# An adaLN block on eight cores: the first K tile summed chunk by chunk, the modulation rows sent through memory, and the opening loads in another order

## The chip, the cores and the metric

The kernel runs on the 8 cores of one Trainium2 chip. Each core computes one element of the batch with the same program, and nothing passes between cores. The metric is the device time of the slowest core in microseconds (us). Engines are TensorE (PE), VectorE (DVE), ScalarE (ACT), GpSimd (POOL) and SyncE (SP, which only starts transfers here). An MiB below is 1.049 MB.

## The reference, cut to what matters

```python
mod = (silu(c) @ wmod).reshape(8, 6, 1, 1024)
sa, ca, ga, sb, cb, gb = mod[:, 0], ..., mod[:, 5]
ga = sign(ga) * maximum(abs(ga), 0.25)          # gb likewise, sign(0) = 1
h = layernorm(x) * (1 + ca) + sa                # x: 2048 tokens of 1024 per core
q = relu(h @ Wq.T) / 8; k = relu(h @ Wk.T) / 8; v = h @ Wv.T; u = silu(h @ Wu.T)
kv = k.T @ v                                    # per head, 16 heads of 64, over all tokens
x = x + ga * ((rms(q @ kv) * u) @ Wo.T)
h = layernorm(x) * (1 + cb) + sb
x = x + gb * (quantised(h) @ quantised(weight).T * scales + bias)
```

## The kernel before, in words

The 2048 tokens are 16 groups `g` of 128 and four tiles `i` of 512. Work goes in this order: an opening (modulation vectors `sa`, `ca`, and the first tile), then K and V for tiles 0 to 3 with the product `kv` (the first phase), then Q, U, the head outputs and the quantising of the FFN weight for tile 0 (`xunit(0, n)`), and then a loop over the 16 groups with Wo, the second norm and the FFN, in which the next tile's Q and U are mixed in.

No scheduler is at work: each engine has a list (`Queue`) that is filled in program order, and each instruction waits on the semaphores in its `after` arguments. So an instruction that waits holds back all that stands behind it on its engine, and a transfer that waits holds back the later ones of SP or POOL. SP's transfers share one queue, POOL's another. The weights are f32 in memory and are cast to bf16 on the way by POOL's transfers.

The parts that the change touches:

- **Opening.** SP loads eight pieces `wa` of 1 MiB (the `sa` and `ca` columns of wmod for one chunk `dc` of 128 features). `wa_sum(dc)` takes two products with accumulation on DVE. POOL loads x. `xhat(g)` normalises a group: statistics, variance plus epsilon and reciprocal on DVE, square root on ACT, minus mean times 1/std on DVE, then `xh` on ACT. `transp(i, c)` turns it on PE into banks 2 and 3, and an eviction applies `ca`, `sa` into `h1`. For tile 0 the eviction only copies, and `scale(dc)` on DVE applies them when the sums are there.
- **K and V.** `kproj(i, hf, j)` is one unit: 8 matmuls 128x512 over the chunks into one of three banks 4, 5, 6, and an eviction on ACT. Tile 0 takes eight such units, then `transp(1, c)`, then tile 1. `vproj` is the same for V, `kvprod` multiplies into banks 0 and 1.
- **Modulation rows.** `ga`, `sb`, `cb`, `gb` come from 16 pieces of wmod of 1 MiB (`mod_piece`, four for each row), through three stage buffers. DVE sums each piece into `accb`, scaled by a column `silc`. `mod_row` then adds over the partitions with an f32 matmul with ones into bank 7, which also spreads the row over all partitions. The same stage buffers carry Wo (`wo_piece`, which folds `ga` in) and the FFN weight (`ffn_quant`). The list `mods` holds these pieces, and one is taken after every second unit of the first phase and one after every unit in its last eight.
- **Late rows.** `last_rows` and `last_row` make gb times bias, and gb times the weight's scales, the latter with f32 matmuls in the group loop after group 0.

## Time and profile before

| what | value |
|---|---|
| median of three runs | 508.58 us (508.37 to 510.7) |
| profiled execution, device time | 510.15 us |
| its span on the slowest core (core 0) | 508.1 us |
| spans of the other seven cores | 499.9 to 504.5 us |
| granted TensorE clock, core 0 | 0.966 of full speed |
| busy: PE, DVE, ACT, POOL | 405.4, 299.4, 237.8, 57.7 us |
| read from and written to memory | 68.26 MB, 24.64 MB |

A core's span runs from its first to its last instruction. The profiled execution's own time is 2.05 us above the span. Busy is not the same as bounding: what matters is which wait ends last in a stretch, and it changes from stretch to stretch.

### The profile page before, as it was taken

The page shows a single profiled execution, that of the slowest core. Times are in us where ns is not written, and L with a number is a line of the kernel's source. Part 1 is how long each engine was busy: PE and PEld are TensorE (multiplying, and loading weights), DVE is VectorE, ACT ScalarE, POOL GpSimd, SP SyncE. Part 2 cuts the span into 40 slices and gives each one's busy share as a digit, 9 for nine tenths or more (in the row PEclk, how much of TensorE's full clock was granted, in tenths as well). Part 3 has the DMA queues.
Part 4 walks back from the last instruction along what each step waited for, and adds up shares of the span by engine and source line. Part 5 has one row for each costly group of instructions (what it writes and reads, how often), then busy time and mean ns, then how long its engine had stood idle before and what let it go on. Part 6 is the DMA issues. An engine that isn't in the chain of part 4 may idle for free.

```text
span 508.1 us, 6419 instructions; the slowest of 8 cores (499.9 to 508.1 us)
## 1 busy us (share of the span) xinstructions
PE 405.4 (80%) x2028; PEld 189.4 (37%) x2068; DVE 299.4 (59%) x524; ACT 237.8 (47%) x348; POOL 57.7 (11%) x90
## 2 busy tenths in 40 slices
PE   0004568968989999787796989998999989998984
PEld 0002234424544444433442434443444434444441
DVE  0388550184867627446886456663666637665884
ACT  1134165454457323156756385445764367643431
POOL 1021011020000000000002111111201212011321
PEclk9999996999999999999898899998999989999998
DMA  7999969999956665920229950656335752455686
GB/s 189 336 335 192 268 189 234 215 195 265 304 221 195 248 221 183 306 92 1 83 70 301 318 140 10 124 118 119 54 77 90 159 85 55 111 84 124 88 142 143
DMA packets 17984, 84.92 MB, mean 167 GB/s; under 512 B 2336, under 2 KB 2336, under 8 KB 12832
## 3 DMA queue, kind: packets, MB, share of 16 engines
q0 software_dynamic: 7776, 32.51, 33.8%
q1 hardware_dynamic: 10176, 52.01, 31.4%
q8 instruction: 17, 0.28, 0.2%
q14 instruction: 15, 0.12, 0.1%
HBM read 68.26 MB, written 24.64 MB: 183 GB/s over the span
## 4 chain that ended last, share of the span: by engine, by line
PE 51%; DVE 19%; ACT 12%; issue 11%; DMA 4%; POOL 1%; DVEq 1%; SPq 1%; ACTq 0%; POOLq 0%
PE pb L315 43%; DVE junk L454 4%; DVE bn L266 3%; DMA wa<-wmod_a 3%; ACT rn L619 2%; PE pb L380 2%; ACT osq L609 2%; DVE h L705 2%; DMA stage<-wmod_b 1%; DVE am L708 1%; PE pb L617 1%; PE pb L343 1%; ACT xq L719 1%; DVE wm_c L424 1%; ACT rn L622 1%
## 5 line engine op out<-in xcount | busy, mean ns | idle before, releaser
L315 PE MATMUL pb<-wk_s,h 128*128 128x512 bf16 x249 | 62.0, 405 | 9.1 <-DVE h L463 5.8
L315 PE MATMUL pb<-fq,xqT 128*128 128x512 bf16 x247 | 60.5, 385 | 3.4 <-ACT xqT L731 2.2
L315 PE MATMUL pb<-wo_s,u_s 128*128 128x512 bf16 x254 | 61.2, 394 | 1.5 <-DVE u_s L599 1.4
L315 PE MATMUL pb<-h,wu_s 128*128 128x512 bf16 x248 | 60.5, 385 | 0.3
L315 PE MATMUL pb<-h,wq_s 128*128 128x512 bf16 x250 | 60.2, 384 | 0.2
L315 PE MATMUL pb<-wv_s,h 128*128 128x512 bf16 x249 | 59.3, 386 | 0.4
L285 PE MATMUL pb<-id_b,xh 128*128 128x128 bf16 x128 | 13.3, 260 | 49.5 <-ACT xh L275 47.9
L624 DVE SCALAR_TENSOR_TENSOR q_s<-rn,pb 128x512 bf16<-128x512 f32 x32 | 22.0, 687 | 44.6 <-ACT rn L622 42.1
L315 PEld LDWEIGHTS pb<-wk_s,h 128*128 128x128 bf16 x256 | 25.9, 103 | 43.2 <-issue 18.4
L371 DVE SCALAR_TENSOR_TENSOR accb<-stage,silc,accb 128x1024 f32<-128x1024 f32 x28 | 36.0, 1285 | 8.9 <-DMA stage<-wmod_b 6.5
L315 PEld LDWEIGHTS pb<-wo_s,u_s 128*128 128x128 bf16 x256 | 25.7, 101 | 33.4 <-issue 6.4
L338 ACT CAST vT<-pb 128x512 bf16<-128x512 f32 x32 | 18.6, 583 | 41.8 <-PE pb L315 41.8
L330 ACT ACTIVATE kT<-pb 128x512 bf16<-128x512 f32 x32 | 18.7, 592 | 41.1 <-PE pb L315 41.1
L315 PEld LDWEIGHTS pb<-h,wq_s 128*128 128x128 bf16 x256 | 25.2, 99 | 30.4 <-issue 2.5
L315 PEld LDWEIGHTS pb<-fq,xqT 128*128 128x128 bf16 x256 | 24.4, 99 | 31.6 <-issue 6.7
L315 PEld LDWEIGHTS pb<-h,wu_s 128*128 128x128 bf16 x256 | 25.1, 99 | 28.9 <-issue 1.1
L584 ACT ACTIVATE q_s<-pb 128x512 bf16<-128x512 f32 x24 | 14.2, 593 | 45.3 <-PE pb L315 43.8
L315 PEld LDWEIGHTS pb<-wv_s,h 128*128 128x128 bf16 x256 | 24.7, 99 | 28.4 <-issue 3.1
L719 ACT ACTIVATE xq<-h,cst,rs 128x1024 f16<-128x1024 f32 x16 | 19.8, 1239 | 22.4 <-DVE rs L713 22.4
L285 PEld LDWEIGHTS pb<-id_b,xh 128*128 128x128 bf16 x128 | 10.5, 117 | 53.0 <-issue 51.1
L454 DVE SCALAR_TENSOR_TENSOR junk<-wa,silr 128x1024 f32<-128x1024 f32 x16 | 19.6, 1224 | 17.4 <-DMA wa<-wmod_a 16.6
L693 POOL TENSOR_SCALAR ve<-m 128x1 f32<-128x1 f32 x6 | 3.3, 550 | 208.5 <-DVE m L690 208.5
(92 smaller groups left out, 561.1 us busy)
## 6 DMA issues: line engine op xcount, KB each, us to landing
stage<-wmod_b SPq DMA_DIRECT2D x16, 1024.0 KB, 7.0
xr<-x_tm POOLq DMA_DIRECT2D x16, 512.0 KB, 16.6
wa<-wmod_a SPq DMA_DIRECT2D x8, 1024.0 KB, 22.2
xr<-x_tm SPq DMA_DIRECT2D x16, 512.0 KB, 3.6
out_tm<-row_gbb SPq DMA_DIRECT2D x4, 2048.0 KB, 20.1
out_tm<-xr POOLq DMA_DIRECT2D x15, 512.0 KB, 8.1
out_tm<-h POOLq DMA_DIRECT2D x15, 512.0 KB, 5.5
stage<-wo SPq DMA_DIRECT2D x4, 1024.0 KB, 14.0
```

Of the source, the lines that this page charges most:

```text
L266: t = DVE.do(lambda e, hf=hf: e.bn_stats(out=bn6[j][:, 6 * hf:6 * hf + 6], in_=x[:, 512 * hf:512 * hf + 512]), x_tok[g])
L285: tp = PE.do(lambda e, d=d, dc=dc, j=j: e.transpose(out=bank[:, 512 * d + 128 * j:512 * d + 128 * j + 128], in_=xh[j][:, 128 * dc:128 * dc ...
L315: t = PE.do(lambda e, dc=dc: e.matmul(pb[bank][:], lhs(dc), rhs(dc), start=(dc == 0), stop=(dc == NC - 1)), *after, each(dc) if each else ...
L330: k_tok[i, j] = ring["free"][b] = ACT.do(lambda e: e.activation(out=kbuf(i, j)[:, 512 * hf:512 * hf + 512], in_=pb[b][:], func=AF.Relu, sc ...
L338: v_tok[i, j] = ring["free"][b] = ACT.do(lambda e: e.copy(out=vT[j][:, 512 * hf:512 * hf + 512], in_=pb[b][:]), t, kv_tok.get((i - 1, j)))
L371: t = DVE.do(lambda e, d=d, dc=dc: e.scalar_tensor_tensor(out=accb[:], in0=s[:, 1024 * d:1024 * d + 1024], scalar=silc[:, dc:dc + 1], in1= ...
L380: t = PE.do(lambda e: e.matmul(pb[7][:], on_f[:], accb[:, sl], start=True, stop=True), t_acc[0], t_ones, b7[0])
L454: t = DVE.do(lambda e, col=col, k=k: e.scalar_tensor_tensor(out=junk[:], in0=wa[dc][:, D * k:D * k + D], scalar=1.0, in1=silr[:], op0=ALU. ...
L584: q_tok[i, ec] = ring["free"][b] = ACT.do(lambda e: e.activation(out=q_s[:, ec], in_=pb[b][:], func=AF.Relu, scale=0.125), t, vp_tok[NT - ...
L609: osq_tok[n] = ACT.do(lambda e: e.activation(out=osq[n % 2][:], in_=pb[b][:], func=AF.Square, scale=UP), o_tok[i, p], s_tok.get(n - 2), kv ...
L624: ot_tok[n] = o_free[b] = DVE.do(lambda e: e.scalar_tensor_tensor(out=q_s[:, p], in0=rn[n % 2][:], scalar=1e12, in1=pb[b][:], op0=ALU.min, ...
L719: xq_tok[g] = ACT.do(lambda e: e.activation(out=xq[a][:], in_=h2[g % 4][:], func=AF.Identity, scale=rs[a][:, 0:1], bias=halfc), am_tok[g], ...
```

## The change

It has these parts:

1. **K of tile 0 chunk by chunk.** `k_first` keeps six units open in banks 4, 5, 6, 0, 1 and 7, and for each chunk `dc` issues one matmul into each of them. The first three transposes of tile 1 stand before chunk 7. The last two units follow as before. Wk has a layout by chunk and comes in eight transfers of 0.5 MiB read each.
2. **Loads.** SP loads x groups 0 to 7 and `wa` alternately. Groups 5, 6, 7 have buffers of their own (`xe`) in the unused part of `h1`. POOL loads only Wk at the start, without a wait. Groups 13, 14, 15 (with both halves of Wq) are queued one block of eight units earlier.
3. **1/std on POOL.** Three small POOL instructions (plus epsilon, power -0.5, minus mean times it) take the place of three DVE and one ACT instruction in `xhat`. Transposed chunks 2, 3, 6 and 7 of tile 1 are evicted by DVE.
4. **Rows through memory.** wmod is laid out so that `mod_piece` takes the same product with accumulation as `wa_sum`, which gives a column [128, 8]. `mod_fin` treats the column, `put` writes it to memory (4 KB in all), and `get` reads it back spread over 128 partitions (512 KB). The f32 matmuls, `accb` and `last_rows` go. Wo's pieces now stand after `sb`'s pieces. The FFN weight is laid out by rows, so `ffn_transp` evicts to every eighth column of `fq`.
5. **silu(c)** is spread over partitions by two small f32 matmuls instead of a 512 KB transfer.

```diff
-    for g in range(4):
-        load_x(POOL, g, g, ())
-    load_w("wk", wk, 0, wa_tok[4])
-    load_w("wk", wk, 1)
+    for dc in range(NC):
+        load_x(SP, dc, dc, ())
+        wa_tok[dc] = SP.dma(sl_a[dc], wa[dc][:], ...)
+    for dc in range(NC):
+        load_wk(dc)
...
-        t = DVE.do(lambda e: e.tensor_scalar_add(out=rt[j][:], in0=mv[j][:, 1:2], scalar1=1e-5),
-                   t, xh_tok.get(g - 4))
-        t = DVE.do(lambda e: e.reciprocal(out=rt[j][:], in_=rt[j][:]), t)
-        t = ACT.do(lambda e: e.activation(out=rt[j][:], in_=rt[j][:], func=AF.Sqrt), t)
-        t = DVE.do(lambda e: e.scalar_tensor_tensor(out=nmr[j][:], ...), t)
+        t = POOL.do(lambda e: e.tensor_scalar(out=rt[j][:], ...), t, xh_tok.get(g - 4))
+        t = POOL.do(lambda e: e.tensor_tensor(out=rt[j][:], in0=rt[j][:], in1=mhalf, op=ALU.pow), t, t_mh)
+        t = nm_tok[g] = POOL.do(lambda e: e.tensor_scalar(out=nmr[j][:], ...), t)
...
+    def k_first(units):
+        units = list(zip((4, 5, 6, 0, 1, 7), units))
+        last = {}
+        for dc in range(NC):
+            if dc == NC - 1:
+                for c in range(3):
+                    transp(1, c)
+            for b, (hf, j) in units:
+                last[b] = PE.do(lambda e, b=b, hf=hf, j=j, dc=dc: e.matmul(
+                    pb[b][:], h1[:, 0, dc, 128 * j:128 * j + 128], wk[:, dc, 512 * hf:512 * hf + 512],
+                    start=(dc == 0), stop=(dc == NC - 1)),
+                    ev_tok[0, dc], w_tok["wk", dc], t_silr, inc=(dc == NC - 1))
...
-        t = PE.do(lambda e: e.matmul(pb[7][:], on_f[:], accb[:, sl], start=True, stop=True),
-                  t_acc[0], t_ones, b7[0])
...
+    def put(k, col, *after):
+        put_tok[k] = SP.dma(sl_p[k], bass.AP(d_rows, k * D, [[NC, 128], [1, NC]]), col[:], *after)
+
+    def get(k, row, *after):
+        row_tok[k] = SP.dma(sl_g[k], row[:], bass.AP(d_rows, k * D, [[0, 128], [1, D]]),
+                            put_tok[k], *after)
+
+    def piece_after(v, k):
+        mod_piece(v, 0)
+        get(k, ROWS[k])
+
+    mods = [lambda c=c: mod_piece(0, c) for c in range(4)]
+    mods.append(lambda: mod_fin(0))
+    for v in (1, 2, 3):
+        mods.append(lambda v=v: piece_after(v, v - 1))
+        mods += [lambda v=v, c=c: mod_piece(v, c) for c in range(1, 4)]
+        mods.append(lambda v=v: mod_fin(v))
+        if v == 1:
+            mods += [lambda c=c: wo_piece(c) for c in range(4)]
+    mods.append(lambda: get(3, row_gbb))
...
-            out=fq[:, :, 128 * ec:128 * ec + 128],
+            out=fq[:, :, ec::NC],
```

Three places where the order changes. On SP, before, from the fourth stage load to the eighth (the names on the right are the tensors in memory):

```order
L44 DMA stage_49<-wmod_b 128x2048
L44 DMA stage_50<-wo 128x2048
L44 DMA stage_51<-wo 128x2048
L44 DMA stage_49<-wo 128x2048
L44 DMA stage_50<-wo 128x2048
```

And on SP after the change, from the same load on (`rows` is the new tensor in memory, `mod_c` the columns):

```order
L44 DMA stage_49<-wmod_b 128x2048
L44 DMA rows<-mod_c_95 128x8
L44 DMA stage_50<-wmod_b 128x2048
L44 DMA row_g<-rows 128x1024
L44 DMA stage_51<-wmod_b 128x2048
L44 DMA stage_49<-wmod_b 128x2048
L44 DMA stage_50<-wmod_b 128x2048
L44 DMA rows<-mod_c_96 128x8
L44 DMA stage_51<-wo 128x2048
```

A write and a read back now stand between the stage loads, so a stage load behind them waits for the row's last sum, and the loads behind the read wait for the write as well.

On POOL after the change, from the end of the opening (group 7's three small instructions, then the transfers of x group 8, Wv, groups 9, 10, Wv's second half, group 11, group 8's small instructions, group 12 and Wu):

```order
L298 TENSOR_SCALAR nmr_125<-mv_117,rt_121 128x1
L44 DMA xr_60<-x_tm 128x1024
L44 DMA wv_s<-wv 128x4096
L44 DMA xr_61<-x_tm 128x1024
L44 DMA xr_57<-x_tm 128x1024
L44 DMA wv_s<-wv 128x4096
L44 DMA xr_58<-x_tm 128x1024
L295 TENSOR_SCALAR rt_118<-mv_114 128x1
L297 TENSOR_TENSOR rt_118<-rt_118,cst 128x1
L298 TENSOR_SCALAR nmr_122<-mv_114,rt_118 128x1
L44 DMA xr_59<-x_tm 128x1024
L44 DMA wu_s<-wu 128x4096 x2
```

Before, POOL had no arithmetic in this phase, and group 8 and the first half of Wv were queued during the opening. Now they stand behind group 7's statistics.

On DVE after the change, from tile 1's evictions to the first row's end (`bn` is the statistics of groups 8 to 11, `stage` the products of the first row's pieces):

```order
L327 TENSOR_SCALAR h_43<-pb,ca_105,sa_c 128x512 x4
L292 BN_STATS bn_0_110<-xr_60 128x6 x2
L292 BN_STATS bn_1_111<-xr_61 128x6 x2
L418 SCALAR_TENSOR_TENSOR stage_49,mod_c_95<-stage_49,silr 128x1024 x2
L292 BN_STATS bn_2_112<-xr_57 128x6 x2
L292 BN_STATS bn_3_113<-xr_58 128x6 x2
L418 SCALAR_TENSOR_TENSOR stage_50,mod_c_95<-stage_50,silr 128x1024 x2
L418 SCALAR_TENSOR_TENSOR stage_51,mod_c_95<-stage_51,silr 128x1024 x2
L439 TENSOR_SCALAR sgn_c<-mod_c_95 128x8
L441 SCALAR_TENSOR_TENSOR abs_c<-sgn_c,mod_c_95 128x8
```

The statistics of groups 10 and 11 stand behind the first piece, as they did before; rows of `bn_aggr` and the fourth piece are between these. The statistics of groups 12 and 13 come only after the seventh piece, those of 14 and 15 after the eighth.

## Rows read from the trace of the kernel before

**Rows 1.** Page: DMA share in 40 slices of 12.7 us.
```profile
DMA  7999969999956665920229950656335752455686
```

**Rows 2.** Busy time by stage, core 0: stretch, engines, granted clock, DMA share, GB/s.
```profile
19.00:56.50 37.50, 7.19 (x39) 3.89 (x39) 30.92 (x72) 10.91 (x13) 4.25 (x8) 1.00 1.00 286
56.50:81.90 25.40, 18.97 (x90) 9.57 (x93) 9.51 (x30) 14.28 (x23) 3.72 (x7) 0.87 0.81 220
81.90:97.30 15.40, 15.35 (x62) 6.59 (x63) 0.00 (x0) 5.48 (x9) 0.00 (x0) 0.88 1.03 212
97.30:121.20 23.90, 19.48 (x111) 9.80 (x112) 15.22 (x27) 10.98 (x18) 3.14 (x5) 0.93 1.00 225
121.20:139.80 18.60, 16.75 (x111) 8.88 (x111) 13.59 (x17) 9.25 (x15) 0.00 (x0) 1.00 0.96 277
139.80:156.90 17.10, 14.42 (x73) 6.53 (x72) 12.05 (x28) 9.52 (x16) 0.00 (x0) 1.00 0.45 165
...
215.70:262.20 46.50, 38.59 (x205) 17.76 (x209) 32.53 (x61) 29.37 (x42) 0.00 (x0) 0.96 0.13 51
```

**Rows 3.** Timeline of DVE and PE in the opening: start, us, instruction, idle before.
```profile
19.03 1.23 DVE L454 SCALAR_TENSOR_TENSOR junk<-wa,silr 128x1024 f32<-128x1024 f32 x1 [16.60 <-DMA wa<-wmod_a]
21.82 1.29 DVE L266 BATCH_NORM_STATS2 bn<-xr 128x6 f32<-128x512 f32 x2
23.53 0.15 DVE L269 TENSOR_SCALAR rt<-mv 128x1 f32<-128x1 f32 x1
56.45 4.85 PE L315 MATMUL pb<-wk_s,h 128*128 128x512 bf16 x11 [2.67 <-DVE h L463]
```

**Rows 4.** Timeline of PE at tile 1's transposes.
```profile
76.92 1.55 PE L285 MATMUL pb<-id_b,xh 128*128 128x128 bf16 x13 [2.41 <-ACT xh L275]
```

**Rows 5.** DMA in one stretch: share, GB/s (the second column is the length).
```profile
12.70:25.40 12.70, 1.00 0.99 337
66.80:84.20 17.40, 0.75 0.88 256
```

**Rows 6.** Wk's two transfers: issue and landing.
```profile
L44 POOL DMA_DIRECT2D wk_s<-wk x2: 535/541/547, 32.2 to 32.7; - x2
DMA to landing us min/median/max: 14.0/17.4/20.8
```

**Rows 7.** POOL's small instructions in the second norm: count, busy, mean ns.
```profile
L695 POOL TENSOR_TENSOR r<-ve,cst 128x1 f32<-128x1 f32 x16 | 12.2, 765 | 2.4
L693 POOL TENSOR_SCALAR ve<-m 128x1 f32<-128x1 f32 x6 | 3.3, 550 | 208.5 <-DVE m L690 208.5
```

**Rows 8.** Timeline of PE at the f32 matmuls of the rows.
```profile
123.40 1.08 PE L380 MATMUL pb<-accb,on_f 128*128 128x512 f32 x2
127.16 1.89 PE L315 MATMUL pb<-wv_s,h 128*128 128x512 bf16 x7
165.60 1.08 PE L380 MATMUL pb<-accb,on_f 128*128 128x512 f32 x2
168.55 3.62 PE L315 MATMUL pb<-wv_s,h 128*128 128x512 bf16 x16
204.18 1.10 PE L380 MATMUL pb<-accb,on_f 128*128 128x512 f32 x2 [1.42 <-DVE accb L371]
207.95 1.89 PE L315 MATMUL pb<-wv_s,h 128*128 128x512 bf16 x7
276.04 1.24 PE L815 MATMUL pb<-accb,on_f 128*128 128x512 f32 x2
281.55 2.88 PE L315 MATMUL pb<-h,wq_s 128*128 128x512 bf16 x8
```

**Rows 9.** DMA issues of the page: KB each, median us to landing.
```profile
blk<-blocks_bf SPq DMA_DIRECT2D x1, 32.0 KB, 12.1
c_s<-c_col SPq DMA_DIRECT2D x1, 4.0 KB, 1.7
```

**Rows 10.** The eviction of the turned FFN weight, 215 to 262 us.
```profile
L444 ACT ACTIVATE fq<-pb,cst 128x1024 bf16<-128x1024 f16 x7 | 7.8, 1113 | 1.5 <-PE pb L440 1.4
```

More of the change, by code:

```diff
@@ L332, in kproj @@
             t, kv_tok.get((0 if i == 2 else i - 1, j)) if i != 1 else None)
+    k_free = {}
+    def k_first(units):
[10 more added lines that the diff above has]
+                    ev_tok[0, dc], w_tok["wk", dc], t_silr, inc=(dc == NC - 1))
+        for b, (hf, j) in units:
+            k_tok[0, j] = k_free[b] = ACT.do(lambda e, b=b, hf=hf, j=j: e.activation(
+                out=kT[j][:, 512 * hf:512 * hf + 512], in_=pb[b][:], func=AF.Relu, scale=0.125), last[b])
+        for b in ring["banks"]:
+            ring["free"][b] = k_free[b]
+        b7[0] = k_free[7]
+        transp(1, 3)
     def vproj(i, hf, j):
@@ L503, in build_nc @@
     eight = [(hf, j) for hf in range(2) for j in range(4)]
-    for n, (hf, j) in enumerate(eight):
+    k_first(eight[:6])
+    for hf, j in eight[6:]:
         kproj(0, hf, j)
-        if n >= 4:
-            xhat(n)
     for g in (9, 10):
```

247 lines of the change are left out of this document (116 added, 131 removed).

## The prediction, on record before the run

> **What bounds the kernel now.** I read the stages first, then the opening's timeline, then TensorE's waits, then what the DMA engines carried. By stage [rows 2] the core is bound by different things. Up to 56.5 us VectorE works through `wa_sum`, `xhat` and `scale` (30.9 busy of 37.5 us) and PE stands nearly idle; the first K matmul that has all its chunks starts at 56.45 [rows 3]. From 56.5 to 81.9 PE does K of tile 0 and then waits for groups 4 to 7, whose chain goes DVE, ACT, DVE, ACT; the last such wait is 2.41 us at 76.92 [rows 4]. K of tile 1 takes to 97.3. V of tile 0 takes 23.9 us with 19.5 busy, tile 1's V 18.6, tile 2's K 17.1. From 215.7 to 262.2 DVE (32.5) and ACT (29.4) share the bound with PE. The group loop after that is mostly PE. Beside all this the DMA engines are full for the first 140 us but for one gap, and slack only after 215 us [rows 1, 2]. That is the second resource to watch: an engine that gets faster asks for its data earlier.
>
> **Price of a transfer.** With f32 loads alone the core moves 337 GB/s [rows 5], 3.11 us per MiB. Wk's halves are counted by the 1 MiB written but read 2 MiB: the second lands at 32.7 + 20.8 = 53.5, the first at 32.2 + 14.0 = 46.2 [rows 6], 7.3 us apart with other loads beside them, against 6.2 for 2 MiB read. So I price every load by what it reads. In the first half's 14.0 us the core could read 4.5 MiB and POOL's queue got 2: about 45% while both queues have work.
>
> **Opening.** It now reads x groups 0 to 7 (4 MiB), `wa` (8) and Wk (4): 16 MiB, 49.8 us from about 5, so the last `wa` lands near 55. Before, Wk began only at 32. The Trainium skill (DMA: Bandwidth & Descriptors, Issuing engines are not separate DMA queues) says that transfers of all engines run on the same 16 DMA engines and interleave, which speaks against this step. The trace agrees: of the two halves of Wk, each took a share of what SP had in flight. By that rule alone a Wk started early delays `wa` by up to 12.4 us.
>
> DVE per chunk: `wa_sum` 21.82 - 19.03 = 2.79 us, statistics 23.53 - 21.82 = 1.71 [rows 3] without the three small ones after them, `scale` about 0.4: 4.9 us against 4.7 us of loads (1.5 MiB). The two are nearly level. With Wk taking 45% until about 33 us, `wa` 2 lands at 30, and then DVE is always a little behind: the last statistics end at 56, `wa_sum(7)` 58.8, the last `scale` 59.6. Before it was 56.6. So the opening itself loses 3 us. The six-bank sums of chunks 0 to 6 (42 matmuls) lie under that wait, even at half clock.
>
> **Tile 1's chain.** POOL's three: power 0.77, the others up to 0.55 [rows 7], with hand-overs 2.3 us; `xh` is 1.24. Group 7 is ready at 59.6. Three transposes (1.0 us each at the low clock), an eviction between, 6 matmuls at half clock 2.6, the fourth transpose, two units of 1.73: K of tile 0 ends at 69.8. Tile 1's K, 8 x 1.73 = 13.8, ends at 83.6, where before it was 97.3: 13.7 us won. The low clock is in the rows: 0.87 granted over 56.5 to 81.9 [rows 2], 4.85 us for 11 matmuls at 56.45 [rows 3].
>
> **V of tile 0 and tile 1.** `xhat` no longer sends DVE to ACT and back, so ACT's evictions aren't held. 8 x 1.73 and three `kvprod` of 0.45 make 15.2 us instead of 23.9. Tile 1's V loses the row's matmuls: 127.16 - 123.40 = 3.76 us with their waits [rows 8], of which 1.6 us show up in 18.6 against 17.0. K of tile 2 could start at 116 instead of 139.8: up to 24 us ahead.
>
> **The giveback.** Group 8 and Wv's first half now wait for group 7's statistics: the DMA engines stand idle from 55 to 59.5. From there POOL queues 16 MiB up to group 15 (groups 8 to 15, both halves of Wv, Wu, Wq), and group 15 is last. DVE reaches group 12's statistics only behind seven stage pieces and group 15's behind eight, so SP moves 8 pieces and the first row (0.5 MiB): 24.5 MiB, 76 us if never idle. Group 15 lands at 136, `xh` is there at 141, and tile 3's first transpose follows at 145.4; in between ACT, waiting in order for groups 12 to 15, holds K of tile 2's evictions. Before that transpose was at 158.6: 24 us have shrunk to 13.2. Before, the DMA engines had their gap near 66 us and were full again to 140 [rows 1]; now 2.5 MiB more (group 8, half of Wv, 7.8 us) stand behind a gap that ends 7 to 10 us earlier. So the loads are hardly ahead of where they were, and PE wants to be 24 us ahead.
>
> **The rest of the first phase.** Rows `sb`, `cb`, `gb` lose their matmuls: `gb` 207.95 - 204.18 = 3.8 [rows 8] and the wait before it 1.4; `sb` 168.55 - 165.60 = 2.9, `cb` the same: 11.0 together. So tile 0's Q starts at 215.7 - 13.2 - 11.0 = 191.5. The stage queue must keep up, since DVE evicts Q behind all rows: 12 pieces from 138 (37.3 us), two read-backs (3.1), 3 of latency, and one drained queue at `put(2)` (6) end at 187.5, products and `mod_fin` at 191. Just in time, with no slack.
>
> **Write and read back.** No row shows a write of 4 KB. Nearest below is the 4 KB load, 1.7 us; above, 12.1 for a small load behind others [rows 9]. I take 3, since the queue is empty when it goes. The read-back moves 0.5 MiB into SBUF, 1.6 us of traffic, and nobody waits for it soon. The Trainium skill (DMA: Bandwidth & Descriptors, Specifications) wants runs of at least 512 B; these are 32 B. No row here shows what that costs.
>
> **FFN weight.** ACT's eviction, 1.11 us [rows 10], now writes every eighth bf16. ACT has about 1.1 us free in each 2.85 us of that stretch, where DVE is the bound, so up to 2.2 us each costs nothing.
>
> **Late row.** From 276.04 to 281.55 PE did two pairs of f32 matmuls and waited for DVE between them [rows 8]: 5.5 us go. The DVE work of `last_rows` (some 3 us) lay beside PE's; no gain taken.
>
> **Sum.** 24.2 + 5.5 = 29.7, less about 0.7 for DVE late at Q: 29. The profiled execution's 510.15 becomes 481.2; its span and the 2.05 us around it move together. It stood 1.6 us above the median of the runs shown, 508.58, so: 480.
>
> **Rivals.**
> - *The loads arrive in time.* POOL's queue gets more than half, group 15 comes by 127 and the 24 us hold until Q. Then only the stage queue binds (187.5 less some overlap): Q at 186, 475. For it: Wk's second half took 7.3 us with others beside it. Against: the byte count.
> - *Mixed loads are slower.* In 66.8 to 84.2, with SP and POOL both loading, the core moved 256 GB/s [rows 5]. Halfway to 337, 296 GB/s is 3.54 us per MiB: 24.5 x 0.43 = 10.5 us later at group 15, 6 more for the 14 MiB behind it. Q at 208, gain 8 + 5.5: 495. Against: part of that stretch was start-up.
> - *ACT's strided eviction.* At 3.3 us each it costs 8 x 1.1 = 9 us: 489. The Trainium skill (SBUF — State Buffer, Specifications (TRN2), Cachelines) says that each access to a new 16-byte line pays; here every element is in a new line. Twice 1.11 is free, three times is this case. No row shows a strided write.
> - *Slower than before.* SP's write and its wait sit in front of the stage loads at four rows, three of them on the path (first, third, last). At 15 us each instead of 3 they cost 36 us: 516. It decides from 13 us each. For it: 12.1 behind other loads. Against: 1.7, and the queue in front is empty.
> - *No gain*, the early loads starving `wa` so that the opening ends beyond 85 us: the traffic would have to fall to 200 GB/s read, which no f32 stretch shows.
>
> **How the numbers follow.** Forecast 480: 0.50. In time 475: 0.17. Mixed slower 495: 0.20. Strided 489: 0.06. Slower 516: 0.04. No gain: 0.03. The forecast's own range, from the transfer shares and the clock, is 472 to 487. With 475 and 495 inside: 469 to 497, which leaves out about 0.12. A measurement of this kernel tells about 0.5% from no change: faster 0.93, same 0.03, slower 0.04.
>
> **What would show it.** Last `scale` at 59 to 61 us. K of tile 1 done at 82 to 86. V of tile 0 in 15 to 16 us. The DMA share at 1.0 from 60 to 135, and PE waiting on ACT inside K of tile 2, ACT in turn on POOL's `nmr` for groups 12 to 15, for 10 us or more. Tile 3's transposes at 140 to 150. Q at 188 to 196. `fq` evictions under 2.2 us. If K of tile 2 has no such wait, the giveback is wrong and it is under 475; if stage loads end after 195, it is over 485.

## The result, and the profile after

The changed kernel takes 525.77 us (median of four runs, 522.57 to 526.32) against 509.32 for the kernel before on the same chip (four runs, 508.37 to 510.7). The ratio is 1.031, with a 95% interval of 1.026 to 1.036: slower. The forecast was 480 with a range of 469 to 497 and 0.04 for slower. The profiled execution took 522.57, its span is 521.0 on core 0, and the rows below are of that core. Executions in which one die ran at a lower granted clock are left out of every time and ratio below; kernel 17 has two left, and no interval.

The stages of the changed kernel, in the columns of [rows 2] (length, then busy time of PE, weight loads, DVE, ACT, POOL, then granted clock, DMA share, GB/s):

```profile
65.10:90.30 25.20, 23.51 (x124) 11.46 (x124) 4.89 (x10) 12.22 (x20) 7.02 (x15) 0.93 0.89 194
90.30:107.40 17.10, 15.38 (x90) 7.56 (x89) 9.82 (x18) 9.34 (x13) 6.42 (x11) 1.00 1.01 282
107.40:124.80 17.40, 17.40 (x132) 9.84 (x130) 3.06 (x8) 10.20 (x17) 0.00 (x0) 1.00 1.02 220
124.80:161.70 36.90, 16.79 (x76) 7.14 (x74) 16.68 (x30) 8.83 (x12) 5.83 (x12) 0.72 0.74 220
...
209.00:281.40 72.40, 46.53 (x213) 20.30 (x211) 34.78 (x68) 54.28 (x41) 0.00 (x0) 0.83 0.30 102
281.40:521.00 239.60, 217.71 (x1074) 98.45 (x1072) 147.09 (x244) 128.98 (x179) 44.09 (x62) 0.98 0.60 130
```

The rows are, in order: from the last `scale` to the end of K of tile 1, V of tile 0, V of tile 1, K of tile 2, the stretch of Q and U of tile 0, and the group loop. Three lengths matter. K of tile 2 is 36.9 us where it was 17.1 [rows 2]. Q and U of tile 0 take 72.4 us, and before it was 46.5. The loop is 6.3 us shorter (239.6 against 508.1 - 262.2 = 245.9). Q starts at 209.0 where it started at 215.7. So 6.7 + 6.3 = 13.0 us were won and 25.9 lost, and the span grew by 12.9. Core 0 is the slowest of eight, and not in all things typical: Q starts at 203.7 to 209.0 on the eight cores of this execution, 206.1 in the mean, against 213.0 in the mean before.

The loss is in one group of instructions, the eviction of the turned FFN weight, to be held against [rows 10]:

```profile
L494 ACT ACTIVATE fq<-pb,cst 128x1024 bf16<-128x1024 f16 x8 | 38.4, 4803 | 4.6 <-PE pb L490 4.6
```

It takes 4.80 us each instead of 1.11. ACT is busy for 54.28 of the 72.4 us, and was 29.37 of 46.5 before. TensorE waits for it seven times there, 19.0 us in all, as at 245.43, and its own work takes longer beside these waits: 46.53 us busy at a granted clock of 0.83, before 38.59 at 0.96. The same timeline of PE shows the other wait, 20.11 us inside K of tile 2:

```profile
65.03 2.68 PE L377 MATMUL pb<-wk_s,h 128*128 128x512 bf16 x6 [3.17 <-DVE h L511]
...
90.35 10.52 PE L346 MATMUL pb<-wv_s,h 128*128 128x512 bf16 x48
...
152.40 9.45 PE L346 MATMUL pb<-wk_s,h 128*128 128x512 bf16 x32 [20.11 <-ACT kT L362]
...
209.02 3.62 PE L346 MATMUL pb<-h,wq_s 128*128 128x512 bf16 x16
...
245.43 1.01 PE L490 MATMUL pb<-id_h,wi 128*128 128x128 f16 x8 [5.07 <-ACT fq L494]
```

That wait is followed back through ACT, POOL and DVE. The timelines at its end, of ACT, of POOL and of DVE:

```profile
150.53 1.24 ACT L301 ACTIVATE xh<-xr,nmr,rt 128x1024 bf16<-128x1024 f32 x1 [23.17 <-POOL nmr L298]
```

```profile
149.05 0.22 POOL L295 TENSOR_SCALAR rt<-mv 128x1 f32<-128x1 f32 x1 [45.41 <-DVE mv L294]
```

```profile
115.57 0.17 DVE L444 SCALAR_TENSOR_TENSOR mod_c<-sgn_c,abs_c 128x8 f32<-128x8 f32 x1 [0.47 <-DVE abs_c L443]
...
132.05 1.23 DVE L418 SCALAR_TENSOR_TENSOR stage<-stage,silr 128x1024 f32<-128x1024 f32 x1 [16.31 <-DMA stage<-wmod_b]
...
142.03 1.22 DVE L418 SCALAR_TENSOR_TENSOR stage<-stage,silr 128x1024 f32<-128x1024 f32 x1 [7.61 <-DMA stage<-wmod_b]
...
147.22 1.28 DVE L292 BATCH_NORM_STATS2 bn<-xr 128x6 f32<-128x512 f32 x2
```

ACT waits for POOL, POOL for the statistics of group 12, and those stand on DVE behind `stage` pieces that land at 132, 142 and 145. Group 12 itself had landed at 99.6 (the issues of POOL's transfers and their times to landing), group 15 at 103.1 + 38.3 = 141.4. So the piece, not the group, holds the first `xh`. SP's timeline shows why the piece is late:

```profile
78.53 16.25 SPq L44 DMA_DIRECT2D stage<-wmod_b  x4
115.81 0.33 SPq L44 DMA_DIRECT2D rows<-mod_c  x1
116.19 0.45 SPq L44 DMA_DIRECT2D stage<-wmod_b  x1
124.47 0.33 SPq L44 DMA_DIRECT2D row_g<-rows  x1
124.85 9.98 SPq L44 DMA_DIRECT2D stage<-wmod_b  x3
```

The first stage load goes at 78.5, behind Wv's first half; the fifth stands behind the row's write, which waits until 115.8 for the row's last sum. The write lands 8.6 us later, beside full DMA engines (share 1.00 in these 9 us; the writes at 152.8 and 187.9 took 1.4 and 1.7 at shares around them of 0.06 and 0.13). The read-back and all later loads of SP wait for it. What that costs is another matter: POOL's loads keep the engines full meanwhile, at 0.96 to 1.04 in every stretch from 78.5 to 141.4.

### The profile page after: what moved, and what is told of

The parts are those of the page before. It is cut to its first block, busy times and chain, and to the rows that moved or that the text cites. A ratio compares the mean times of both kernels' runs of the same rounds, so it can differ in the third digit from the quotient of the medians.

```text
span 521.0 us, 6388 instructions; the slowest of 8 cores (515.3 to 521.0 us)
## 1 busy us (share of the span) xinstructions
PE 402.7 (77%) x2052; PEld 187.2 (36%) x2052; DVE 277.9 (53%) x492; ACT 258.9 (50%) x327; POOL 82.6 (16%) x136
## 4 chain that ended last, share of the span: by engine, by line
DMA 31%; PE 30%; ACT 15%; DVE 12%; issue 7%; POOL 2%; SPq 2%; DVEq 0%; ACTq 0%; POOLq 0%
PE pb L346 26%; DMA stage<-wmod_b 16%; ACT fq L494 6%; DMA wa<-wmod_a 6%; DVE stage L418 3%; DMA stage<-ffn_w 3%; DMA wv_s<-wv 2%; SPq L44 2%; DMA stage<-wo 2%; ACT rn L665 2%; DMA rows<-mod_c 2%; DVE h L751 1%; ACT osq L655 1%; DVE bn L292 1%; DVE am L754 1%
## 5 line engine op out<-in xcount | busy, mean ns | idle before, releaser
L418 DVE SCALAR_TENSOR_TENSOR stage<-stage,silr 128x1024 f32<-128x1024 f32 x32 | 37.9, 1221 | 62.4 <-DMA stage<-wmod_b 62.2
L346 PE MATMUL pb<-h,wu_s 128*128 128x512 bf16 x256 | 66.7, 410 | 0.0
L346 PE MATMUL pb<-wk_s,h 128*128 128x512 bf16 x208 | 48.3, 393 | 20.5 <-ACT kT L362 20.1
L346 PE MATMUL pb<-h,wq_s 128*128 128x512 bf16 x256 | 62.2, 388 | 0.0
L346 PE MATMUL pb<-wo_s,u_s 128*128 128x512 bf16 x256 | 58.6, 380 | 1.4 <-DVE u_s L645 1.4
L301 ACT ACTIVATE xh<-xr,nmr,rt 128x1024 bf16<-128x1024 f32 x13 | 16.1, 1240 | 60.2 <-POOL nmr L298 60.2
L494 ACT ACTIVATE fq<-pb,cst 128x1024 bf16<-128x1024 f16 x8 | 38.4, 4803 | 4.6 <-PE pb L490 4.6
L346 PEld LDWEIGHTS pb<-wk_s,h 128*128 128x128 bf16 x208 | 20.6, 100 | 46.1 <-issue 24.4
L645 DVE TENSOR_TENSOR u_s<-q_s,u_s 128x512 bf16<-128x512 bf16 x32 | 13.6, 425 | 38.2 <-ACT u_s L642 38.2
L346 PEld LDWEIGHTS pb<-wv_s,h 128*128 128x128 bf16 x256 | 24.3, 98 | 26.2
L739 POOL TENSOR_SCALAR ve<-m 128x1 f32<-128x1 f32 x6 | 5.5, 917 | 169.7 <-DVE m L736 169.7
L765 ACT ACTIVATE xq<-h,cst,rs 128x1024 f16<-128x1024 f32 x16 | 19.8, 1240 | 21.9 <-DVE rs L759 21.9
```

The lines of the kernel that those rows point to most:

```text
L301: xh_tok[g] = x_free[g] = ACT.do(lambda e: e.activation(out=xh[j][:], in_=x[:], func=AF.Identity, scale=rt[j][:, 0:1], bias=nmr[j][:, 0:1] ...
L346: t = PE.do(lambda e, dc=dc: e.matmul(pb[bank][:], lhs(dc), rhs(dc), start=(dc == 0), stop=(dc == NC - 1)), *after, each(dc) if each else ...
L418: st_free[n] = col_tok[v] = DVE.do(lambda e, d=d: e.scalar_tensor_tensor(out=s[:, D * d:D * d + D], in0=s[:, D * d:D * d + D], scalar=1.0, ...
L494: b7[0] = fq_tok[ec] = ACT.do(lambda e: e.activation(out=fq[:, :, ec::NC], in_=bank.rearrange("p (c o) -> p c o", c=NC), func=AF.Identity, ...
L645: ou_tok[i, ec] = DVE.do(lambda e: e.tensor_tensor(out=u_s[i % 2][:, ec], in0=q_s[:, ec], in1=u_s[i % 2][:, ec], op=ALU.mult), ot_tok[8 * ...
L765: xq_tok[g] = ACT.do(lambda e: e.activation(out=xq[a][:], in_=h2[g % 4][:], func=AF.Identity, scale=rs[a][:, 0:1], bias=halfc), am_tok[g], ...
```

## The experiments

Each ran beside the kernel before on the same chip, and ratios are to that kernel. The chips differ between kernels, so kernels are best compared by their ratios (0.01 is about 5 us). Kernels called "mixed" compute the FFN with its output channels in an order that the rows don't follow. The edits are against the changed kernel unless another is named.

**1. The eviction writes contiguous columns (mixed).**

```diff
-            out=fq[:, :, ec::NC],
+            out=fq[:, :, 128 * ec:128 * ec + 128],
```

> The changed kernel with one line undone: ScalarE's eviction of the turned FFN weight writes 128 columns in a row instead of every eighth (so the FFN's output channels come out in another order than the rows that scale them). Theory S (the strided write costs 4.8 - 1.1 us, eight times, on the chain): evictions back to 1.11 us, the stretch of tile 0's Q and U back from 72 to about 46.5 us, the whole at 525.8 - 26 = 499 to 501 us, 2% below the kernel before. Theory O (the stretch is long because VectorE comes to it late and the modulation rows hold it): the evictions shorten but the stretch keeps more than 60 us and the whole stays above 515.

It took 499.44 us (497.6 to 500.11), ratio 0.975 (0.972 to 0.979). The evictions are back at 1.11 us each, and Q and U of tile 0 take 46.5 us (210.4 to 256.9). The 26 us are the strided write, and no other part of the change: by time it is 26.3 us less than the changed kernel, by the two ratios 28, give or take 3.

**2. The strided write put into the kernel before, and nothing else of the change (mixed).**

> The kernel before with that one line of the change done alone: the eviction writes every eighth column (channels in another order). Theory S: +25 to +27 us, 534 to 537 us, and the stretch of tile 0's Q and U about 72 us instead of 46.5. Theory O: under +10 us, since here VectorE and the rows are as before.

It took 538.52 us (535.0 to 539.15), ratio 1.051 (1.046 to 1.056), which is 26 us more than the kernel before:

```profile
L444 ACT ACTIVATE fq<-pb,cst 128x1024 bf16<-128x1024 f16 x8 | 38.4, 4805 | 5.2 <-PE pb L440 5.2
```

The cost needs nothing else of the change. From both sides it is 26 us.

**3. Contiguous, and the last two rows laid out to match** (whole computation). Their writes become runs of one f32:

```diff
-        put_tok[k] = SP.dma(..., bass.AP(d_rows, k * D, [[NC, 128], [1, NC]]), ...)
+        dst = [[NC, 128], [1, NC]] if k < 3 else [[1, 128], [128, NC]]
+        put_tok[k] = SP.dma(..., bass.AP(d_rows, k * D, dst), ...)
```

> The whole computation with a contiguous eviction: gb's columns, the bias and the FFN weight are laid out as feature 128c + p instead of 8p + c, and the two rows that belong to them are written to memory in runs of 4 bytes (1024 of them) instead of 32. Theory S: within 1 us of the run with the one line undone, 499 to 502, since these two writes are waited for by nobody on the path. Rival: short runs are dear; each of the two writes takes over 10 us, the read-back of bias times gb comes late and the x and FFN loads queued behind it on SyncE delay the FFN weight: 505 or more.

It took 521.55 us (519.63 to 526.86), ratio 1.021 (1.013 to 1.029). Its DMA issues (KB each, median us to landing):

```profile
rows<-mod_c SPq DMA_DIRECT2D x3, 4.0 KB, 1.4
rows<-gbb_c SPq DMA_DIRECT2D x1, 4.0 KB, 14.7
rows<-gws_c SPq DMA_DIRECT2D x1, 4.0 KB, 17.2
```

The same 4 KB take 1.4 us in runs of 32 bytes and 14.7 or 17.2 in runs of 4. On SP the read-back, five x loads and the FFN weight's loads stand behind the first of them, so these loads go at 231 us instead of about 215. TensorE then has two long waits that kernel 1 doesn't have, 23.2 us together, which is what lies between the two ratios:

```profile
250.06 0.59 PE L656 MATMUL pb<-q_s,kv_bd 128*128 128x512 bf16 x1 [15.10 <-DVE q_s L673]
...
310.16 0.59 PE L656 MATMUL pb<-q_s,kv_bd 128*128 128x512 bf16 x1 [8.10 <-DVE q_s L673]
```

The rival is right.

**4 to 7. One edit of the order each, on kernel 3.** The rows' writes and reads one or two stage loads later (4); groups 12 to 15 of x queued ahead of Wq and Wu (5); 5, and their statistics one by one between the units of V of tile 1 (6); no wait of the stage loads for Wv's first half, with x in its old place (7). So 6 has two edits.

> On top of the version with the contiguous eviction and the right layout: each write of a row to memory is queued on SyncE behind the second next stage load, its read-back behind the third, so no stage load waits for a row's last sum. Theory W (the 20 us that TensorE waits inside K of tile 2 come from stage loads held at the first row's write and read-back): that wait falls by 8 us or more and the whole is 6 to 12 us faster than without the edit. Theory C (they come from the small share that the stage loads get beside GpSimd's casting loads): the wait falls by under 4 us and the whole by under 4.

> On top of the contiguous version: GpSimd queues x groups 12 to 15 ahead of Wu and Wq, which come after them, and nothing else moves. Theory D (the wait inside K of tile 2 stands because VectorE reaches the statistics of groups 12 to 15 only behind stage pieces 5 to 8): groups 12 to 15 land by 115 us and the wait stays, unless the later casting loads free the stage loads in 85 to 125 us, which gives at most 6 us. My forecast (group 15 lands last of 16 MiB): the wait falls from 20 us to under 5 and the whole by 12 or more.

> As the run with x first, and the statistics of groups 12 to 15 stand on VectorE before stage pieces 5 to 8 (the normalising on ScalarE keeps its place). Theory D: the wait inside K of tile 2 is gone (under 2 us), Q of tile 0 starts some 15 us earlier unless the stage pieces, now the only thing late, hold it: total 6 to 16 us below the contiguous version. Theory C alone: no more than with x first.

> On top of the contiguous version: the stage loads no longer wait for the first half of Wv, only for the opening's sums. Theory G (the DMA engines stand idle or half used from 60 to 80 us because SyncE waits at that gate, and all stage pieces are that much late): the first stage load goes at 64 instead of 78 us, the wait in K of tile 2 falls by 8 us or more. Rival: the stage loads then share with Wv, which lands later than V of tile 0 wants it (over 90 us), and nothing is won.

| kernel | time, us | ratio (95%) | waits in K of tile 2, slowest core (mean of eight), us | Q of tile 0, slowest core (mean of eight) |
|---|---|---|---|---|
| 3, the base | 521.55 | 1.021 (1.013 to 1.029) | 20.9 (19.4) | 208.7 (207.2) |
| 4 writes later | 510.62 | 1.002 (0.999 to 1.005) | 12.1 and 6.4 (19.1) | 211.5 (207.8) |
| 5 x first | 525.17 | 1.031 (1.025 to 1.037) | 24.0 (21.4) | 209.0 (207.6) |
| 6 and statistics | 521.0 | 1.024 (1.018 to 1.030) | 16.5 (15.4) | 208.0 (202.7) |
| 7 no wait for Wv | 520.2 | 1.024 (1.016 to 1.032) | 13.5 (13.3) | 205.3 (204.7) |

Kernel 4 gained about 10 us, but not where it was meant to: Q is no earlier. The first of the two slow writes now goes at 195.7 and its read-back at 213.2, where kernel 3 has 212.0 and 226.8, so the FFN weight's loads go at 217.4 instead of 231.2, and the wait of 15.1 us becomes 3.8. Inside K of tile 2 it is no clean test of the row's write: that write took 15.1 us there, and the eighth stage piece still stood behind its read-back. Sending x first, alone, gains nothing, so the landing of group 15 isn't the bound by itself. In kernel 7 another wait came, as its rival has it: 5.4 us in V of tile 0. Kernels 6 and 7 bring Q forward by 4.5 and 2.5 us in the mean of the cores, and nothing of it is left in the time. None of the four removes the wait.

**8. The last two rows turned on TensorE** into [8, 128] by a small f32 matmul with the identity, and written in runs of 512 bytes (whole computation).

> The after kernel with the FFN weight's output channels laid out so that the eviction of the turned weight writes 1024 contiguous bf16 again, and with the whole computation kept: the two rows that belong to these channels (gb times bias, gb times weight scale) are turned on TensorE from a column [128, 8] to [8, 128] by one small f32 matmul with the identity, and then written in runs of 512 bytes. Theory S (the strided eviction is the whole loss of the Q/U stretch, 4-byte runs were what cost the first layout): evictions 1.1 us, the two writes land in under 3 us each, the x loads behind them are not late, and the time is that of the wrong-order contiguous kernel, 499.4 plus at most 1: 499 to 502. Rival W (any write and read-back at this place of SP's queue delays the loads of the group loop, whatever its runs): writes fast, loop start 260 or later, 508 to 512.

It took 518.14 us (517.46 to 519.19), ratio 1.018 (1.014 to 1.022). Rival W holds in kind, by my own placing of it, and its 508 to 512 was too low. The matmul stood at Q's tenth unit, in SP's order ahead of the FFN weight's last two loads:

```profile
204.45 3.85 SPq L44 DMA_DIRECT2D stage<-ffn_w  x2
250.14 0.29 SPq L44 DMA_DIRECT2D rows<-colT  x1
251.52 0.34 SPq L44 DMA_DIRECT2D row_gbb<-rows  x1
251.91 0.90 SPq L44 DMA_DIRECT2D stage<-ffn_w  x2
```

The write itself is fast (1.4 us from issue to the read behind it). The two loads behind it go at 251.9, and in kernel 1 the last of the four went at 236.3 on its slowest core. It doesn't tell whether the turn is a good way, only that the place was wrong.

**9. Kernel 8 with all edits of the order together**, the four groups' statistics now in one block ahead of a stage piece.

> The kernel of the run before it (contiguous eviction, rows turned on TensorE) with the order changed in four places: the rows' writes stand two stage loads later and the reads another one later, the stage loads do not wait for Wv's first half, groups 12 to 15 of x are queued ahead of Wq and Wu, and their statistics stand in front of the stage pieces of that block instead of between them. Theory B (bytes: what must come before group 15's use is the same 24 MiB as before less 4 MiB of Wq and Wu) expects the wait inside K of tile 2 to shrink from about 20 us to 8 or less, Q at 200 or sooner, and 490 to 496. Rival P (DVE catches up elsewhere: with the stage pieces later, the stage queue binds at Q): the wait goes, but Q stays at 207 to 210 and the time at 498 to 502. The single edits on the 4-byte layout moved Q by 1.0 (x first), 2.0 (statistics) and 4.7 us (no gate).

It took 506.86 us (505.02 to 509.64), ratio 0.994 (0.992 to 0.997). The wait in K of tile 2 is gone and Q starts at 189.5, but TensorE then waits 11.8 us for DVE's eviction of Q, and the FFN weight is late as in kernel 8. B is right on the wait and on Q's start (200 or sooner), but not on the time. P's stage queue does bind at Q, as that wait of 11.8 us, though Q starts long before 207. The time is above what either had, with kernel 8's late loads still in it.

**10. Kernel 1 (mixed) with x first and all four groups' statistics in one block.**

```diff
+        if n == 3:
+            for g in range(12, 16):
+                xhat(g, late=True)
...
```

> The kernel with the contiguous eviction alone (FFN channels in another order than the row's, 499.4 us) plus two edits together: groups 12 to 15 of x queued ahead of Wq and Wu, and all their statistics in front of the stage pieces of that block. Each alone did little. Theory C (two things each late enough to hold the wait: group 15 lands late, and DVE reaches its statistics behind stage pieces that are themselves late): together they take the wait in K of tile 2 from 20 us to under 8, tile 3's K starts at 168 or sooner; Q then only as early as the stage pieces allow, 200 to 206, and 492 to 496. Rival (transfers were the bound for both, the bytes only change places): the wait is still 15 us or more in sum, or comes back one for one as a wait on a stage piece; 498 to 500.

It took 495.08 us (493.82 to 495.5), ratio 0.972 (0.969 to 0.975). TensorE's timeline:

```profile
184.13 3.62 PE L355 MATMUL pb<-h,wq_s 128*128 128x512 bf16 x16
...
209.32 0.58 PE L669 MATMUL pb<-q_s,kv_bd 128*128 128x512 bf16 x1 [21.57 <-DVE q_s L642]
```

No wait of 1 us is left in K of tile 2 on any core, and Q starts at 184.1. In the mean of the eight cores that is 183.4, 23 us ahead of kernel 1's 206.9. Then nearly all of it comes back: DVE, in order, works through the last row's pieces before it casts `kv` and evicts Q. On the same core it takes these pieces at 192.07 (waited 7.36 us for its landing), 197.93 (3.48), 200.42 and 202.91. Theory C is right on the wait, its rival right on the sum: 20 us became a wait on a stage piece. By time 4.4 us stayed, but the two kernels ran on different chips. By their ratios, 0.972 and 0.975, it is 1.8 us, give or take 2.4, which can't be told from nothing.

**11. A ruler of steps (mixed).** Two evictions write at a step of 2 elements, four at 4, and one each on ACT and DVE is contiguous.

> A ruler, not a version: in the after kernel the eight evictions of the turned FFN weight write other places, so that the FFN's channels are mixed. Two write at a step of 2 elements (4 bytes), four at a step of 4 (8 bytes), one contiguous on ScalarE, one contiguous on VectorE. Known: step 1 takes 1.11 us, step 8 (16 bytes) 4.80. Theory L (cost goes by 16-byte lines: two or more elements in each line are free): 1.1 us at step 2 and at step 4. Theory T (any step breaks a fast path, one price): 4.8 at both. Theory P (in proportion to the bytes spanned): 1.1 to 2.2 at step 2, 2.2 to 3 at step 4.

One run, 500.79 us. The timelines of ACT and of DVE:

```profile
239.53 1.39 ACT L502 ACTIVATE fq<-pb,cst 128x1024 bf16<-128x1024 f16 x1
...
245.49 2.54 ACT L502 ACTIVATE fq<-pb,cst 128x1024 bf16<-128x1024 f16 x1
...
259.25 1.11 ACT L502 ACTIVATE fq<-pb,cst 128x1024 bf16<-128x1024 f16 x1 [0.48 <-PE pb L490]
```

```profile
261.96 0.68 DVE L499 TENSOR_SCALAR fq<-pb 128x1024 bf16<-128x1024 f16 x1
```

Steps of 1, 2, 4 and 8 elements (2, 4, 8 and 16 bytes) cost 1.11, 1.39, 2.54 and 4.80 us. From 2 to 4 it is 1.15 more and from 4 to 8 it is 2.26: theory P. From a step of 4 bytes on, the cost grows in proportion, about 0.28 us for each byte of step in 1024 elements; between 2 and 4 bytes it is half of that. Steps beyond 16 bytes weren't tried. The Trainium skill (SBUF — State Buffer, Specifications (TRN2), Cachelines) gives 16-byte lines that want two or more hits for full bandwidth. By that, the step of 4, which puts two elements in a line, would be free, and the step of 2 with its four the more so. Here they cost 2.3 and 1.25 times the contiguous write, so the measurement decides.

**12. The step of 8, half of it on DVE** (whole computation).

> The after kernel with every second eviction of the turned FFN weight on VectorE, at the same step of 8 elements. VectorE took 0.68 us for a contiguous one, ScalarE 1.11 contiguous and 4.80 at step 8. Theory M (the price is that of writing bf16 16 bytes apart into on-chip memory, whoever writes): VectorE about 4.4 to 4.8 us. Theory S (ScalarE's own): VectorE 0.7 to 1.4 us. The time would be 525.8 less what the four faster ones free: about 520 under M, 508 to 514 under S.

One run, 532.05 us. The two engines' groups:

```profile
L496 DVE TENSOR_SCALAR fq<-pb 128x1024 bf16<-128x1024 f16 x4 | 18.7, 4683 | 0.0
L499 ACT ACTIVATE fq<-pb,cst 128x1024 bf16<-128x1024 f16 x4 | 19.2, 4801 | 16.5 <-PE pb L490 16.5
```

Theory M: DVE pays 4.68 us where it took 0.68. The price isn't ScalarE's. My figure of 520 was wrong: sharing the evictions out made the stretch longer. Neither engine is full in it (DVE is busy for 51.1 of the 82 us from 205, ACT for 40.1), but TensorE waits 25.2 us for the evictions, 15.1 of them for DVE's, where it waited 19.0 for ACT's alone. DVE, in order, also makes the weight's pieces and Q's products there; how much each of these was held wasn't separated.

**13. Kernel 3 with the last two rows on POOL's queue**, idle there (whole computation).

```diff
-        put_tok[k] = SP.dma(sl_p[k], ...
+        put_tok[k] = (SP if k < 3 else POOL).dma(sl_p[k], ...
...
```

The read-back of gb times bias goes with them, and that of the last row moves on SP from the head of the loop's loads to behind group 0.

> The after kernel with a contiguous eviction of the turned FFN weight and the whole computation kept, in the first layout (the last two rows are written in 4-byte runs), but with these two writes and the read-back of gb's row on POOL's queue, which has nothing else between 141 us and the group loop; the read-back of the last row stands on SP behind group 0's loads. Theory Q (the 4-byte writes cost 15 to 17 us of latency and nothing else; what cost 22 us was what stood behind them in SP's queue): 499 to 502, the loop starts at 257 to 259. Rival D (a write of a thousand 4-byte runs also slows other transfers, or POOL's own work waits for it): loop start as early, but 503 to 512 from waits in groups 0 to 2.

It took 501.38 us (500.29 to 502.14), ratio 0.981 (0.977 to 0.985). The writes are even slower there, and no engine's work waits for them:

```profile
rows<-gbb_c POOLq DMA_DIRECT2D x1, 4.0 KB, 18.4
rows<-gws_c POOLq DMA_DIRECT2D x1, 4.0 KB, 21.9
```

Theory Q: 20 us between kernels 3 and 13 (ratios 1.021 and 0.981) were the queue behind the write, not the write (with the last read-back out of SP's way too, which wasn't tried by itself). That the writes were slower needn't be POOL's queue: the DMA share beside them was 0.98 and 1.03, beside kernel 3's it was 0.03 and 0.05.

**14. Kernel 13 with the edits of kernel 10.**

> The run before it (rows on POOL's queue) plus groups 12 to 15 of x ahead of Wq and Wu and their statistics ahead of the stage pieces, the edits that gave 495.1 against 499.4 in a kernel with mixed channels. Both theories on the wait in K of tile 2 are settled by that run; this one is the base for the next and should show the same step: 4 to 5 us under the run before it, 494 to 498, Q at 184, its second head's wait at 209 on VectorE.

It took 500.25 us (498.69 to 501.12), ratio 0.980 (0.975 to 0.984). Q starts at 187.8 on its slowest core and waits 22.4 us for DVE. That is 1.1 us under kernel 13, too little to tell from nothing, as in kernel 10.

**15. Kernel 14 with two of the last row's four pieces behind the first Q units** on DVE.

```diff
-        if mods:
+        if n == 1:
             mods.pop(0)()
...
```

> The run before it with two of the four pieces of gb's row, and what follows from them, behind the first Q units in VectorE's order, and the five x loads for the loop behind these pieces in SP's queue. Theory V (with Q's start at 184, VectorE, in order, waits for the last stage pieces that land at 194 and 196 before it casts kv and evicts Q): the wait of 21.6 us at TensorE shrinks by 7 to 10, the loop starts 6 to 9 earlier, 486 to 490. Rival F (the stage buffers and SP's queue are the bound until the FFN weight too, so the time comes back as a wait on the FFN weight's pieces): wait at Q shorter, but the loop's start moves by under 3 us: 492 to 496.

It took 496.58 us (494.59 to 497.89), ratio 0.972 (0.966 to 0.977). On core 5 of the profiled run the wait is 12.9 us instead of 22.0, and the loop starts at 245.6 instead of 257.2; in the mean of the cores it starts 5.0 us sooner (248.3 against 253.3). The time is 3.7 us less, between theory V's 6 to 9 and what rival F leaves. Part of the gain is lost in the loop: DVE waits 6.5 us for the last row's read-back, which stood behind a load on SP.

```profile
199.08 0.58 PE L672 MATMUL pb<-q_s,kv_bd 128*128 128x512 bf16 x1 [12.90 <-DVE q_s L645]
```

**16. Kernel 1 (mixed) with Wk's transfers waiting for the third `wa`.**

> The kernel with contiguous eviction alone and channels in another order (499.4 us), with one edit: Wk's eight transfers wait for the third piece of wa (about 36 us). In the prediction's opening Wk takes 45 percent of the traffic until 33 us and VectorE is then always a little behind. Theory E (Wk started early delays wa; with SP alone at 337 GB/s the pieces come level with VectorE): the last scale at 60 to 62 instead of 65, first K chunks still in time, K of tile 1 ends 3 to 4 us sooner, 496 to 497. Rival N (all 16 MiB must come before 60 us in any order, and the last wa lands at the same time): last scale at 65, 499 or, if Wk's last chunk now comes late, up to 502.

It took 492.89 us (490.98 to 493.94), ratio 0.964 (0.960 to 0.969), some 6 us under kernel 1 by the ratios. Theory E is right on the last `scale`, but most of the gain isn't where it had it. The third `wa` lands at 20.6 us (35.1 in kernel 13), and the last `scale` ends at 60.5, where kernel 13, on the same chip and core, has it at 62.3. But K of tile 1 ends at 85.8 against 86.0 there, where PE came out of a longer wait at the lower clock (0.81 granted from 60 to 70 us, 0.97 there). Core 0 shows least of it: in the mean of the eight cores the last `scale` ends 2.6 us sooner (60.7 against 63.3) and K of tile 1 1.9 us sooner (86.4 against 88.3). More moved in the queue of loads: SP's first stage load goes at 67.5, not 72.4, and the statistics of group 12 come 5.5 us sooner. DVE's timelines, of this kernel first and then of kernel 13:

```profile
59.81 0.73 DVE L512 TENSOR_SCALAR h<-h,ca,sa_c 128x512 bf16<-128x512 bf16 x2
...
122.43 1.22 DVE L419 SCALAR_TENSOR_TENSOR stage<-stage,silr 128x1024 f32<-128x1024 f32 x1 [15.91 <-DMA stage<-wmod_b]
...
136.53 1.28 DVE L293 BATCH_NORM_STATS2 bn<-xr 128x6 f32<-128x512 f32 x2
```

```profile
126.85 1.22 DVE L420 SCALAR_TENSOR_TENSOR stage<-stage,silr 128x1024 f32<-128x1024 f32 x1 [16.26 <-DMA stage<-wmod_b]
...
142.03 1.28 DVE L294 BATCH_NORM_STATS2 bn<-xr 128x6 f32<-128x512 f32 x2
```

The wait in K of tile 2 falls from 21.0 to 15.9 us, and Q starts at 198.1 against 204.4 (199.7 against 205.9 in the mean).

**17. All that helped together** (whole computation), with the last row's read-back ahead of the x loads.

> All that helped, whole computation kept: contiguous eviction, last two rows on POOL's queue, groups 12 to 15 of x and their statistics first, two of gb's pieces behind Q's start, Wk after the third piece of wa, and the read-back of the last row ahead of the loop's x loads on SP (in the run with gb's pieces late VectorE waited 9.2 us for it). Theory A (the parts act at different places, so they add up): 497.2 less 5 for Wk (499.4 to 492.9 there, of which some is the wait in K of tile 2, gone here) less 5 for the read-back: 486 to 490. Rival M (Q's start moves ahead, but the stage pieces of sb, cb and gb land when they land): the wait at Q grows by what the opening gives, and only the read-back's 3 to 5 us stay: 492 to 495.

It took 492.72 and 495.39 us, against 509.97 for the kernel before: 3% faster, without an interval. Q starts at 182.9 and waits:

```profile
200.62 0.58 PE L673 MATMUL pb<-q_s,kv_bd 128*128 128x512 bf16 x1 [14.14 <-DVE q_s L646]
...
298.80 3.57 PE L358 MATMUL pb<-h,wu_s 128*128 128x512 bf16 x8 [4.71 <-DVE h L809]
```

Rival M: the parts don't add up, since the stage pieces land when they land. The second wait, on the FFN's output, was expected to go and is still 4.7 us. The trace shows what holds it. DVE waits for the last row:

```profile
297.91 0.75 DVE L809 SCALAR_TENSOR_TENSOR h<-pb,xs,row_g 128x512 f32<-128x512 f32 x1 [7.67 <-DMA row_g<-rows]
```

The row's slow write goes on POOL's queue at 248.3 and lands 24.3 us later; the read-back, at the head of SP's queue now, waits for it until 272.7 and takes 25.1 us beside full DMA engines (share 1.04), where it took 6.3 in kernel 13. So the write on an idle queue is free only as long as its row isn't the next thing wanted.

## Why the prediction was wrong

In spans it said 508.1 - 29 = 479.1, and it was 521.0. Of the 41.9 us, 25.9 are Q and U of tile 0, and 17.5 are Q's start (209.0, not 191.5). The loop was 0.8 better than said, and 0.7 that the sum took off for DVE at Q goes the other way.

- **The eviction: the mis-sized term that made it slower.** The price was the error: 4.80 us each, eight times, where the sum put nothing and the rival took three times 1.11, which is 3.3, at a chance of 0.06. No row showed a strided write, and I bounded it by what would be free, not by a row. Kernels 1 and 2 put 26 us on it, kernel 11 shows the price by step. "Up to 2.2 us each costs nothing" was too high as well: eight at 4.80 us cost 25.9 us, and in kernel 11, where four take 2.54, the stretch is 3.7 us longer than in kernel 1 (50.7 against 47.0 in the mean of the cores). Both fit a threshold near 1.6 us, an estimate from these two numbers. With this term alone, 480 would have become 506.
- **The opening.** The last `scale` came at 65.1 instead of 59.6, K of tile 1 ended at 90.3 instead of 83.6. The mechanism was foreseen (Wk early delays `wa`, DVE always behind), the size was short: the third `wa` landed at 36.1, not 30. Part of it is the core: the last `scale` ends at 61.8 to 65.1 on the eight cores, 63.2 in the mean, and the same opening gives 61.7 to 65.5 in kernel 1 and 61.9 to 65.0 in kernel 13. Kernel 16 takes Wk's early start away and gets 2.6 us of it back, and 1.9 at the end of K of tile 1 (means against kernel 13). It agrees with the Trainium skill (DMA: Bandwidth & Descriptors, Issuing engines are not separate DMA queues) on `wa`'s landing, 20.6 against 35.1 us; most of what the delay costs comes later, as later loads.
- **V of tile 0** took 17.1 us, not 15.2; 1.7 of it is one wait on ACT. V of tile 1 took 17.4, where 17.0 was said.
- **The giveback: right in kind, and the time of its end the second term that was mis-sized.** K of tile 2 did wait for ACT, and ACT for `nmr` of groups 12 to 15, in all 20 us where 10 or more were named. But group 15's `xh` came at 157.55, not 141. The step that failed is "24.5 MiB, 76 us if never idle", with 5 us from there to `xh`. The loads began at 65.0, not 59.5. The last of these 24.5 MiB, the eighth stage piece, landed at 147.3, where 136 was said: 82.3 us, 3.36 us per MiB instead of 3.11. And from there to `xh` DVE's turn took 10.2 us, since it had the statistics of groups 12 and 13, this piece and groups 14 and 15 still to do, one after another. Group 15 itself had landed at 141.4. The rival "mixed loads are slower" had this best: 3.54 us per MiB and Q at 208, where it came at 209.0. The closeness of its Q is luck in part, since 5.5 us of the lateness are the opening's.
- **Write and read-back.** "I take 3, since the queue is empty" was wrong for the first row: SP's queue was empty and the DMA engines weren't, and it took 8.6 us (8.4 in the median of kernel 9's rows, 15.1 for the first of kernel 4). The rival "slower by write and wait" had the mechanism, at 8.6 us once and 1.4 to 1.7 at the other rows, well under its 13. Whether this write made the wait in K of tile 2 longer isn't shown: the engines were full while SP stood, kernels 4 to 7 don't remove the wait, and kernel 10 removes it with the write in its old place. What it takes is both, the transfer early and DVE's turn early.
- **The stage queue.** "Just in time, with no slack" was the most useful sentence of it. In kernels 10, 14, 15 and 17 Q starts at 183 to 188, near the 186 of the rival "in time", and the stage pieces hold DVE, and TensorE with it, until 199 to 214.
- **The late row** gave 6.3 us against 5.5.

What stays open: how much of the 16.5 us at group 15's `xh` each of the three parts (late start, slower loads, DVE's turn) would give back alone, what a write of the first row at 3 us would have changed, and why the cores of one execution differ by 3 us in the opening. The turn on TensorE at a better place wasn't tried.

## What to carry to other kernels

A change of layout that looks like a matter of bookkeeping sets the step of an on-chip write or the run of a write to memory; find the price of both on the chip before moving other work around it. When a wait is said to go, name the next thing in line on the in-order engine that will be asked earlier: here statistics behind stage pieces, then Q behind stage pieces, gave back all but about 2 of 23 us. A tiny transfer in a queue costs what stands behind it: the same slow write cost 20 us on SP's queue ahead of the FFN weight and nothing on an idle one in kernel 13, until in kernel 17 its own row was the next thing wanted. And read an opening on all cores: the spread between cores was as large as the effect looked for.
